# The first pass of a gated two-layer kernel: TensorE's queue reordered in parts, and the decay exponents as bf16 products over exact terms

## The reference, cut to what matters

```python
log_f = jax.nn.log_sigmoid(fg)
cs = concatenate([0, cumsum(log_f)])
log_d = where(tri, (cs - cs.T)[1:, 1:] + ig.T, neg)   # decay exponents, 64 x 64 a head
m = max(log_d, axis=-1)
d = exp(log_d - m)
c = q @ (k.T / sqrt(dh)) * d
n = maximum(sum(c), exp(-m))
h = c / (n + eps) @ v
```

## Time and profile before

| | |
|---|---|
| median of 3 runs | 593.76 us (592.67 to 594.1) |
| the profiled execution | 595.22 us, its span 593.5 us |
| PE busy | 483.4 us, 81% of the span |
| weight loads busy | 360.7 us, 61% |
| DVE busy | 334.0 us, 56% |
| ACT busy | 307.1 us, 52% |
| POOL busy | 217.3 us, 37% |
| mean granted clock of TensorE | 0.843 |

### The profile page before, as it was taken

The page is one execution under the profiler, slowest core; times in us unless marked ns, Lnnn a source line. Parts: engine busy times, 40 slices in busy tenths (PEclk is TensorE's granted clock), DMA queues, the critical chain, the costliest instruction groups (busy, mean ns, idle before and its releaser), DMA issues. The chain is left out here.

```text
span 593.5 us, 12772 instructions
## 1 busy us (share of the span) xinstructions
PE 483.4 (81%) x3787; PEld 360.7 (61%) x3787; DVE 334.0 (56%) x1455; ACT 307.1 (52%) x764; POOL 217.3 (37%) x210
## 2 busy tenths in 40 slices
PE   0359999999999999984549999999924779888884
PEld 0346778788787877863425777777722456666652
DVE  6223578877787877678423222222213577777872
ACT  1346676656566656531203333333403678888872
POOL 5200114444434444546520000000048888888400
PEclk9998777867677767787558999999975898999997
DMA  5971112222222211140120433443142456666521
GB/s 137 189 165 56 55 56 68 79 72 69 71 67 71 73 54 49 46 120 30 33 70 24 107 107 106 106 106 107 36 119 36 101 98 143 141 142 141 128 88 38
DMA packets 85067, 51.98 MB, mean 88 GB/s; under 512 B 7555, under 2 KB 78886, under 8 KB 85030
## 3 DMA queue, kind: packets, MB, share of 16 engines
q1 hardware_dynamic: 73766, 43.09, 27.0%
q0 software_dynamic: 11264, 8.43, 8.2%
HBM read 26.07 MB, written 16.91 MB: 72 GB/s over the span
## 5 line engine op out<-in xcount | busy, mean ns | idle before, releaser
L666 POOL DMA_INDIRECT s_xs<-slots_y,s_gidx x64 | 98.9, 1545 | 154.4 <-DMA slots_y<-s_ye 135.2
L795 ACT ACTIVATE s_ht<-heads,s_cols 128x512 f32<-128x512 f32 x64 | 44.0, 687 | 85.5 <-PE heads L1036 85.2
L147 ACT ACTIVATE s_xn<-s_xs,s_ln_shift,s_ln_rstd 128x128 f32 (+1 forms) x192 | 77.6, 481 | 16.7 <-DVE s_ln_shift L140 16.6
L99 DVE BATCH_NORM_STATS2 s_ln_stats<-s_xs 128x6 f32 (+1 forms) x256 | 54.7, 279 | 35.3 <-DMA s_xs<-slots_y,s_gidx 20.9
L644 POOL DMA_INDIRECT slots_x<-s_xn,s_sidx x64 | 62.9, 983 | 22.9 <-issue 22.9
L1036 PE MATMUL heads<-s_xet,s_w_sb 128*128 128x512 f32 x128 | 60.6, 618 | 1.7 <-DVE s_xet L1396 1.7
L630 POOL TENSOR_TENSOR s_hs<-s_hs,s_head_w 128x512 f32<-128x512 f32 x16 | 20.3, 1269 | 111.5 <-DVE s_hs L1280 111.5
L1043 PE MATMUL bank<-s_w_sb,s_ht 128*128 128x128 f32 x512 | 59.9, 275 | 0.9 <-DVE s_ye L1405 0.9
L1043 PEld LDWEIGHTS bank<-s_w_sb,s_ht 128*128 128x128 f32 x512 | 58.5, 192 | 1.5 <-issue 1.5
L935 PE MATMUL heads<-s_dec_r,s_dec_l 128*128 128x512 f32 x64 | 52.5, 970 | 0.0
L960 PE MATMUL heads<-s_vaug,s_cw 64*64 64x33 f32 x1024 | 49.3, 267 | 0.1
(11 more groups left out here) (190 smaller groups left out, 946.9 us busy)
## 6 DMA issues: line engine op xcount, KB each, us to landing
slots_x<-s_xe SPq DMA_DIRECT2D x8, 516.0 KB, 11.3
s_xe<-slots_x SPq DMA_DIRECT2D x16, 258.0 KB, 3.1
s_xs<-in_x_dram SPq DMA_DIRECT2D x16, 256.0 KB, 2.9
s_ctxb<-in_ctx_dram SPq DMA_DIRECT2D x16, 256.0 KB, 3.2
s_kpt<-s_kt SPq DMA_DIRECT2D x16, 256.0 KB, 2.4
s_w_sb<-in_L_ffn_w_dram SPq DMA_DIRECT2D x16, 256.0 KB, 3.2
slots_y<-s_ye SPq DMA_DIRECT2D x16, 256.0 KB, 2.3
s_ctxv<-in_ctx_dram SPq DMA_DIRECT2D x16, 256.0 KB, 3.5
```

The lines of the kernel that those rows point to most:

```text
L99: last = dve.bn_stats(self.stats[:, i * GT + t, :], tile(t))
L147: last = act.activation(out(t), tile(t), ACT.Identity, bias=self.shift[:, j:j + 1], scale=self.rstd[:, j:j + 1])
L666: pool.indirect_dma_start(out=xs[:, n * D:(n + 1) * D], out_offset=None, in_=slots_y, in_offset=bass.IndirectOffsetOnAxis(ap=gidx[:, n:n + ...
L795: act.activation(ht[:, s_par, c, :], heads[:, c, :], ACT.Gelu_apprx_tanh, bias=col).then_inc(h_done, 1)
```

## The change

All of it is in the first pass. Four things are done.

- An fp32 number is taken apart into three terms whose top halves (the upper 16 bits of the word, read as bf16 by `top_half`) add up to it: the number, the number less its own top half, and that less its own top half. DVE does this with two subtractions each for a (`am` becomes three times as wide) and for the running maximum (`mrow` has three rows for one).
- The transpose of a yields 48 rows for 16, and the rows of the maxima are six for two, brought by six DMAs for two, of which the first two wait for the maximum, and each next two for a term. The constant rows are laid out anew in POOL's setup. PE multiplies the top halves of dec_l and dec_r as bf16, still with K = 128 and 512 columns.
- PE's order in a step is changed: scores in two parts with the turning of the maxima between them; gate products of two tiles, one and one, between the head values of one tile each; the transposes of the routed rows before the last head values; the decay products apart, with forget sums and the queries' transposes between them.
- The semaphores count the finer parts: l_ps goes up with each decay product, and a_terms and m_terms are new.

```diff
+def top_half(ap):
+    return ap.bitcast(BF16).rearrange("p (n w) -> p n w", w=2)[:, :, 1]
...
             def spread_max(g, half, q):
+                hold(sp, l_ps, nth(g - 2, 2, 2), consts)
                 hold(sp, mrow_done, g + 1, consts)
-                hold(sp, l_ps, g - 1, consts)
-                for b in range(2):
-                    sp.dma_start(dec_r[32 + b:33 + b, q, :], mrow[:, q, b * S:(b + 1) * S]).then_inc(m_in[q], 16)
+                for j in range(3):
+                    if j:
+                        hold(sp, m_terms, nth(g, j, 2), consts)
+                    for b in range(2):
+                        row = 3 * R + 3 * b + j
+                        sp.dma_start(dec_r[row:row + 1, q, :], mrow[:, q, j, b * S:(b + 1) * S]).then_inc(m_in[q], 16)
...
-            step(pool.memset(dec_r[0:R, :, :], 1.0))
-            for q in range(2):
-                step(pool.affine_select(out=dec_r[0:R, q, :], in_=dec_r[0:R, q, :], compare_op=ALU.is_equal, fill=0.0, base=0,
-                                        pattern=[[1, R], [0, S]], channel_multiplier=-1))
+            step(pool.memset(pick[:, :, :], 0.0))
+            for j in range(3):
+                step(pool.affine_select(out=pick[:, :, :], in_=pick[:, :, :], compare_op=ALU.not_equal, fill=1.0, base=-j * R,
+                                        pattern=[[0, 2], [-1, R]], channel_multiplier=1))
+            step(pool.tensor_copy(dec_r[0:3 * R, :, :].rearrange("p q (r i) -> p (q r) i", i=S),
+                                  pick[:, :, :].rearrange("p q r -> p (q r)").unsqueeze(2).to_broadcast([3 * R, 2 * R, S])))
...
             def turn_a(g, half, q):
-                pe.wait_ge(a_done, g + 1)
-                pe.transpose(bank[6][0:R, 128:256], am[:, q, :], ident[:, :]).then_inc(at_ps, 1)
+                hold(pe, a_terms, nth(g, 2, 2), consts)
+                pe.transpose(bank[6][0:3 * R, 128:256], am[:, q, :], ident[:, :]).then_inc(at_ps, 1)
...
-            def decay_exponents(g, half, q):
-                pe.wait_ge(arow_done, g + 1)
-                hold(pe, m_in[q], half * 32 + 32, consts)
-                need(pe, cw_done, nth(g - 1, 2, 2))
-                for u in range(2):
-                    last = pe.matmul(heads[:, u, :], dec_l[:, q, :], dec_r[:, q, u * GW:(u + 1) * GW], start=True, stop=True)
-                last.then_inc(l_ps, 1)
+            def decay_exponents(g, half, q, u):
+                if u == 0:
+                    pe.wait_ge(arow_done, g + 1)
+                    hold(pe, m_in[q], half * 96 + 96, consts)
+                need(pe, cw_done, nth(g - 1, u + 1, 2))
+                pe.matmul(heads[:, u, :], top_half(dec_l[:, q, :]), top_half(dec_r[:, q, u * GW:(u + 1) * GW]),
+                                 start=True, stop=True).then_inc(l_ps, 1)
...
                 if three:
-                    scores(*three)
+                    scores(three[0], three[2], (0, 1))
                 if two:
                     turn_maxima(*two)
+                if three:
+                    scores(three[0], three[2], (2, 3))
                 if six:
                     count_tokens(*six)
                 if one:
-                    gate_products(*one)
+                    gate_products(one[0], one[2], (0, 1))
                 if three:
-                    head_values(*three)
+                    head_values(three[0], three[2], (0,))
+                if one:
+                    gate_products(one[0], one[2], (2,))
+                if three:
+                    head_values(three[0], three[2], (1,))
+                if one:
+                    gate_products(one[0], one[2], (3,))
+                if three:
+                    head_values(three[0], three[2], (2,))
                 if five:
                     turn_routed(*five)
+                if three:
+                    head_values(three[0], three[2], (3,))
                 if two:
-                    decay_exponents(*two)
+                    decay_exponents(*two, 0)
                 if one:
                     forget_sums(*one)
                 if zero:
                     turn_queries(*zero)
+                if two:
+                    decay_exponents(*two, 1)
+                if zero:
                     turn_context(*zero)
                 if one:
                     turn_a(*one)
...
             def a_values(g, half, q):
                 dve.wait_ge(f_ps, g + 1)
                 need(dve, at_ps, g - 1)
-                dve.tensor_tensor(am[:, q, :], gates[:, 0, :], bank[6][:, 64:64 + R], ALU.subtract).then_inc(a_done, 1)
+                dve.tensor_tensor(am[:, q, 0:R], gates[:, 0, :], bank[6][:, 64:64 + R], ALU.subtract).then_inc(a_done, 1)
+                dve.wait_ge(a_done, g + 1)
+                for j in range(2):
+                    if j:
+                        dve.wait_ge(a_terms, nth(g, 1, 2))
+                    term = am[:, q, j * R:(j + 1) * R]
+                    dve.tensor_tensor(am[:, q, (j + 1) * R:(j + 2) * R], term, top_half(term), ALU.subtract).then_inc(a_terms, 1)
...
-                dve.tensor_tensor_scan(mrow[:, q, :], reset[:, :], bank[6][0:R, 128:256], 0.0, ALU.add, ALU.max).then_inc(mrow_done, 1)
+                dve.tensor_tensor_scan(mrow[:, q, 0, :], reset[:, :], bank[6][0:R, 128:256], 0.0, ALU.add, ALU.max).then_inc(mrow_done, 1)
+                dve.wait_ge(mrow_done, g + 1)
+                for j in range(2):
+                    if j:
+                        dve.wait_ge(m_terms, nth(g, 1, 2))
+                    term = mrow[:, q, j, :]
+                    dve.tensor_tensor(mrow[:, q, j + 1, :], term, top_half(term), ALU.subtract).then_inc(m_terms, 1)
```

More of the change, by code:

```diff
@@ L260, in flamingo @@
         logf = sb("logf", [P, R])
-        am = sb("am", [P, 2, R])
-        mrow = sb("mrow", [R, 2, P])
+        am = sb("am", [P, 2, 3 * R])
+        mrow = sb("mrow", [R, 2, 3, P])
+        pick = sb("pick", [3 * R, 2, R])
         em = sb("em", [P, 2, R])
@@ L339, in flamingo @@
         a_done = sem("a_done")
+        a_terms = sem("a_terms")
+        m_terms = sem("m_terms")
         at_ps = sem("at_ps")
@@ L607, in _ @@
                                   ident[S:P, S:P].unsqueeze(1).to_broadcast([S, 4, S])))
[L608 to L612, removed]
+            step(pool.memset(dec_l[32:S, :, :], -1.0))
+            for b in range(2):
+                half = dec_l[32:S, :, b * S:(b + 1) * S]
+                step(pool.affine_select(out=half, in_=half, compare_op=ALU.is_ge, fill=0.0, base=32 - 3 * R - 3 * b,
+                                        pattern=[[0, 2], [0, S]], channel_multiplier=1))
+                step(pool.affine_select(out=half, in_=half, compare_op=ALU.is_ge, fill=0.0, base=3 * R + 3 * b + 2 - 32,
+                                        pattern=[[0, 2], [0, S]], channel_multiplier=-1))
             step(pool.memset(reset[:, :], 0.0))
@@ L900, in turn_queries, with gate_products @@
                 last.then_inc(xt1_done, 1)
[L902 to L909, removed]
+            def gate_products(g, q, tiles_of):
+                if 0 in tiles_of:
+                    if isinstance(g, int) and g == 0:
+                        pe.wait_ge(dve_setup, 1)
+                    pe.wait_ge(kt_done, g + 1)
+                    hold(pe, em_done, g, consts)
+                    pe.wait_ge(qt_done, g + 1)
+                for t in tiles_of:
                     tile = bank[6][:, t * 2 * NH:(t + 1) * 2 * NH]
@@ L912, in gate_products @@
                     last = pe.matmul(tile, qt[:, t * P:(t + 1) * P], kqkv[:, 0, :], start=False, stop=True)
-                last.then_inc(gates_ps, 1)
+                if GT - 1 in tiles_of:
+                    last.then_inc(gates_ps, 1)
             def forget_sums(g, half, q):
@@ L926, in turn_maxima, with scores @@
                 pe.matmul(bank[6][:, 256:256 + R], tri[:, :], logf[:, :], start=True, stop=False)
-                pe.matmul(bank[6][:, 256:256 + R], mrow[:, q, :], ident[0:R, 0:R], start=False, stop=True).then_inc(mt_ps, 1)
-            def decay_exponents(g, half, q):
-                pe.wait_ge(arow_done, g + 1)
-                hold(pe, m_in[q], half * 32 + 32, consts)
-                need(pe, cw_done, nth(g - 1, 2, 2))
-                for u in range(2):
-                    last = pe.matmul(heads[:, u, :], dec_l[:, q, :], dec_r[:, q, u * GW:(u + 1) * GW], start=True, stop=True)
-                last.then_inc(l_ps, 1)
-            def scores(g, half, q):
-                for t in range(GT):
+                pe.matmul(bank[6][:, 256:256 + R], mrow[:, q, 0, :], ident[0:R, 0:R], start=False, stop=True).then_inc(mt_ps, 1)
+            def decay_exponents(g, half, q, u):
[5 more added lines that the diff above has]
+                                 start=True, stop=True).then_inc(l_ps, 1)
+            def scores(g, q, tiles_of):
+                for t in tiles_of:
                     if t == 0:
@@ L947, in scores, with head_values @@
                     last.then_inc(scores_done, 1)
```

(4 more changed lines are left out.)

10 lines of the change are left out of this document (5 added, 5 removed).

## The result

| | before | after |
|---|---|---|
| median | 593.93 us (592.67 to 596.03, 4 runs) | 647.94 us (643.86 to 649.23, 4 runs) |
| ratio | | 1.0894, 95% interval 1.0835 to 1.0953 |
| span of the profiled run | 593.5 us | 647.0 us |
| mean granted clock | 0.843 | 0.772 |
| nine steps of the first pass, mean | 15.35 us | 18.81 us |

The change made the kernel 54 us slower. The forecast was 587.5 us with a range of 575 to 612; the outcome is beyond it, past the third rival (635 us). A few executions of a kernel take 1.5% or more longer than its fastest, whatever the kernel, and the medians and ratios in this document leave them out.

A forecast was written before the change was run, and what follows sets the result against it. PE's queue, at its clock level, was taken to bound the first pass. At a 40% share, 13.8 us of work plus 1.1 of waits made 14.9 us a step against 15.35, 7 us over 15 steps: 587.5 us, range 575 to 612.

The forecast's parts named there:

- third rival: First pass: the clock hardly rises, 18.1 us a step, +2.7 us over 15 steps, 635 us; chance 9%.
- Tw: PE's work for a whole first-pass step at 2.4 GHz: 11.6 us before, 10.3 us with bf16 decay products.
- Tc: PE's work for a whole first-pass step at 1.2 GHz: 20.4 us before, 17.9 us with bf16 decay products.
- the formula: Work done per us: share at 2.4 GHz over Tw plus share at 1.2 GHz over Tc; its inverse is step work.
- The bf16 products: PE's decay products: two cost 0.43 us at 2.4 GHz or 0.87 at 1.2, saving 1.27 or 2.54 us a step.
- The terms on VectorE: Four added subtractions on DVE: 1.0 us a step, making its work, the floor of a step, 13.8 us.
- The six DMAs and the setup: Six DMAs on SP's queue hidden behind PE's work; GpSimd's setup 0, bounds -1 and +1 us once.
- The waits: New or earlier waits, for terms, forget sums and maxima: 1.1 us a step, bounds 0.3 and 2.
- The other order at nothing: PE's new order, gate products between head values: costed at nothing, bounds -0.3 and +0.4 us.
- The clock: Share of first-pass time PE runs at 2.4 GHz: 40% taken, bounds 46% (as before) and 0.
- a rival at 27% and 9%: Clock rises later or half as long: share 20%, 16.2 us a step, 607 us (27%); hardly rises, 635 us (9%).
- The rule on transposes: Skill's rule: the full clock doesn't engage at a PE transpose, which doesn't count as busy; then the third rival's time.

The follow-up runs named there:

- e4: The kernel before plus 28 idle bf16 products of 240 columns a step, ahead of the gate-product and head-value tiles; 604.1 us, ratio 1.018.
- e9: The kernel before with bf16 decay products and terms, and of the new order only the decay products apart; 604.4 us (two runs).
- e7: The kernel before (fp32) with only its two decay products apart, forget sums and the queries' transposes between them; 582.4 us, ratio 0.977.
- e1: The changed kernel with each bf16 decay product issued four times into the same bank; 630.3 us, ratio 1.060 to the kernel before.
- e3: The changed kernel's new order, with fp32 decay products and one term put back; 629.5 us, ratio 1.059 to the kernel before.
- e6: The kernel before (fp32) with only the scores in two halves and the turning of the maxima between them; 618.5 us, ratio 1.039.
- e10: The changed kernel with the scores whole again; 630.1 us, ratio 1.050 to the kernel before.
- e11: The changed kernel with gate products and head values whole, not interleaved; 633.8 us, ratio 1.062 to the kernel before.
- e2: The changed kernel's bf16 products and terms, with the old PE order put back; 595.6 us, ratio 1.001 to the kernel before.

## Why the prediction was wrong, point by point

- **What bounds the pass.** Right: PE's queue at the level of its clock. Tw was a little high (11.6 for 11.2 in e4) and the bf16 Tc a little low (17.9 for the 18.2 of e9's steps at 1.2 GHz). In a mixture near half and half the two errors cancel, so that the formula gave e7 to 0.1 us; for e9 it is up to half a microsecond short.
- **The bf16 products.** Right: 0.43 us each at 1.2 GHz, so 2.5 us a step saved there. Strided top halves stream no slower than the whole bf16 tiles of the earlier trace rows (0.217 us at 2.4 GHz).
- **The terms on VectorE.** Right: 0.97 us for 1.0. Its floor was never reached.
- **The six DMAs and the setup.** Right, nothing: e1 and e3 differ by 0.8 us.
- **The waits.** Too high for the changed kernel: 0.46 us of real idle time a step for 1.1 in the sum. The waits for the maximum come where the scores run at 2.4 GHz, as foreseen, and here they seldom did. Where they do (e6), the split of the scores adds 0.8 us, and I had not seen the second half of it, ScalarE's exponential behind the keys' copy.
- **The other order at nothing.** Wrong. It was bounded by -0.3 and +0.4. By steps at 1.2 GHz throughout, interleaving costs 1.0 us and the split of the scores 0.4 (e9, e10, e11); by the formula, with clock and idle taken out, e3 gives 16.94 - 0.4 - 15.5 = 1.0 and interleaving alone 0.9. The step that failed was to count instructions and not the borders between their shapes. The trace of before had only two borders of head values a step and showed no price by itself.
- **The clock.** Wrong, and the main error. I took a share of 40%, "nearer the upper end, because the rest of the wide work keeps its place"; it was 8%, and the sign that I had named for it, PEclk under 0.64, is what came (0.54). The rows had shown that each rise stood at the end of a decay stretch, and I weighed it as a rival at 27% and 9%. The bf16 products lowered the share in each order tried: 46 to 32% (before, e2), 64 to 26% (e7, e9), 42 to 8% (e3, changed kernel), and in the last of these putting the streaming back restored it (e1).
- **The rule on transposes.** I had cited the Trainium skill ("TensorE: Matmul & The Clock Gate", Part 4: PE-mode transpose) against the forecast. The time came out on its side, but no run here separates transposes from other wide work, so whether they help to raise the clock is neither confirmed nor refuted.

The ledger of one step, from 15.35 us, by the formula: the shorter products at an unchanged clock -1.65 (15.0 to 13.4), the fall of the share from 46 to 8% +3.5 (13.4 to 16.9), and 1.6 that the formula doesn't hold: 18.8. Of the 1.6, about 1.4 is what the steps at 1.2 GHz show for the order against e9's, and 0.3 the formula's Tc, too low; these two estimates are 0.1 too many. The nine steps account for 31.1 of the 53.5 us between the two profiled spans. The six other steps account for 18.0, above all the first ones, which run at 1.2 GHz until 85 us, and the stretch ahead of the first cut for 4.3. Rival 3 had the mechanism; its 18.1 us for a step at 1.2 GHz was 1.5 under the 19.63 measured, by what the order costs and the low Tc.

The two halves of the change don't add: +35 us for the order, 0 for the bf16 products, and 54 for both. The 19 us between them are the clock: with the order in place, e1 against the changed kernel gives 18 us for the same missing streaming, at the same idle time.

## What to carry to other kernels

Where an engine's clock follows its load, don't take a saving in wide products at the price of the stretch it stands in: read what stands ahead of each rise of the clock, and ask what raises it when that is gone. Price each order by its borders between product shapes and by which queue each new, earlier request waits for; try its parts one by one, since here two parts cost 4.5% and 3.9% and the third gained 2.3%. And hold the profile against itself: durations of known instructions against its clock row, counts of products against counts of weight loads.

## What the runs showed of the hardware

- Issuing each of two products four times for once made the kernel 18 us faster (648 to 630 us), with the clock over nine steps from 0.54 to 0.70. Issuing them twice gave most of it (ratios 1.089, 1.066 and 1.060).
- With bf16 fillers of 240 columns the clock was 1.00 in seven of nine steps (mean 0.95, for 0.73); 28 of them cost 3.3 us a step. In the changed order the same 28 didn't hold it (0.59).
- At 1.2 GHz, a tile of eight fp32 products of 64x64 (16 records) took 1.00 us between full-width products and 0.89 among its like, and a tile of two fp32 products of 8 columns (four records) 0.95 and 0.86.
- Equal instructions in a slightly different order ran at a mean clock of 0.73 or 0.82 (before, e7), 1.7 us of 15.35 a step apart over nine steps, 11 us apart over the kernel.
- The clock row read 1.00 up to 83 us in the changed kernel, where decay products took 0.42 us and four transposes 0.85, their durations at 1.2 GHz.
- 16 of 3755 products had no record, and the time of each showed as idle time put down to another engine (0.45 us).
